# Masked attention over 256 keys: diagonal blocks side by side, the full block a product of its own

## The reference

```
L0_attn  scores = q k^T * scale + linear position bias; causal mask; softmax; times v   (16 channels a head)
L2_xattn q, k, v with low-rank additions; causal mask (T = S = 256); softmax; times v   (16 channels a head)
L3_attn  scores = (q_r k_r^T + q_i k_i^T) / sqrt(16); causal mask; softmax; times (v_r, v_i)   (32 a head)
```

## Time and profile before

| what | value |
|---|---|
| median of 3 runs | 3406.8 us (3401.21 to 3409.35) |
| the profiled execution | 3406.46 us |
| its span | 3404.6 us |
| TensorE busy | 2733.6 us, 80% |
| VectorE busy | 1700.3 us, 50% |
| ScalarE busy | 1108.8 us, 33% |
| mean granted TensorE clock | 0.864 |
| L0_attn, L2_xattn, L3_attn: first mask product | 740, 2268, 3044 us |

### The profile page before, as it was taken

One profiled execution on the slowest core, in us unless ns is written; L12 is line 12 of the kernel. 1 busy time (PEld: TensorE's weight loads), 2 busy tenths in 40 slices (PEclk: granted clock), 3 DMA queues, 4 the chain that ended last, 5 costly groups with the idle time before them and its releaser, 6 DMA issues. The chain is left out here.

```text
span 3404.6 us, 39821 instructions
## 1 busy us (share of the span) xinstructions
PE 2733.6 (80%) x15316; PEld 1488.6 (44%) x15320; DVE 1700.3 (50%) x2604; ACT 1108.8 (33%) x1564; POOL 191.8 (6%) x362
## 2 busy tenths in 40 slices
PE   3799599878999967998799759687684668978777
PEld 2233233335555544435343335434222555746446
DVE  5677477522111135774677287423697424322423
ACT  2466356512111112664366226211321113302220
POOL 2000100000000000000000045000000000000000
PEclk8799699987999978999899856798677788979888
DMA  4633443221221125431633000100100241020200
GB/s 156 145 54 50 113 105 57 32 76 38 74 74 70 41 87 131 80 58 21 162 59 58 24 10 1 47 24 1 51 0 0 99 158 52 1 77 1 81 1 7
DMA packets 89492, 202.14 MB, mean 59 GB/s; under 512 B 10770, under 2 KB 66322, under 8 KB 78354
## 3 DMA queue, kind: packets, MB, share of 16 engines
q1 hardware_dynamic: 85566, 184.09, 21.9%
q10 hardware_dynamic: 3750, 15.65, 1.2%
HBM read 171.56 MB, written 28.15 MB: 59 GB/s over the span
## 5 line engine op out<-in xcount | busy, mean ns | idle before, releaser
L589 DVE TENSOR_REDUCE sta_parts<-sta_psS 128x1 f32<-128x1024 f32 x544 | 644.1, 1191 | 250.3 <-PE sta_psS L519 241.8
L648 ACT ACTIVATE sta_probs<-sta_psS 128x1024 f32<-128x1024 f32 x544 | 543.0, 998 | 424.2 <-PE sta_psS L519 421.3
L519 PE MATMUL sta_psS<-L_xattna_kst,L_xattn_qS 99*128 99x512 bf16 x1088 | 339.2, 398 | 67.3 <-DMA L_xattna_kst<-ones_rows 61.3
L531 PE MATMUL sta_psO<-sta_probs,L_xattn_V 128*32 128x256 f32 x4224 | 368.3, 393 | 13.2 <-ACT sta_num L631 10.7
L519 PE MATMUL sta_psS<-L_xattn_qS,L_xattna_kst 99*128 99x256 bf16 x2112 | 325.4, 276 | 23.0 <-DVE L_xattn_qS L599 13.1
L519 PEld LDWEIGHTS sta_psS<-L_xattn_qS,L_xattna_kst 99*128 99x128 bf16 x2112 | 189.4, 98 | 200.2 <-DVE sta_parts L589 82.2
L519 PEld LDWEIGHTS sta_psS<-L_xattna_kst,L_xattn_qS 99*128 99x128 bf16 x1088 | 65.0, 99 | 286.0 <-issue 190.7
L531 PEld LDWEIGHTS sta_psO<-sta_probs,L_xattn_V 128*32 128x32 f32 x4224 | 95.9, 108 | 133.3 <-issue 89.6
L1298 DVE TENSOR_TENSOR l0f_hT<-exp_psG,l0f_gel 128x512 f32<-128x512 f32 x72 | 49.8, 692 | 204.5 <-PE exp_psG L1267 204.5
L199 ACT ACT_TABLE_LOAD x14 | 18.0, 1283 | 368.5 <-PEq L59 368.5
L1283 ACT ACTIVATE l0f_gel<-exp_psA 128x512 f32<-128x512 f32 x72 | 43.0, 597 | 275.5 <-PE exp_psA L1264 275.5
(11 more groups left out here) (578 smaller groups left out, 4312.7 us busy)
## 6 DMA issues: line engine op xcount, KB each, us to landing
L_xattna_kst<-L_xattn_keys SPq DMA_DIRECT2D x192, 136.0 KB
L_xattn_keys<-prt_parts SPq DMA_DIRECT2D x64, 384.0 KB, 2.6
L_xattna_kst<-L_xattn_keys SPq DMA_DIRECT2D x192, 128.0 KB
L_xattn_cx<-in_ctx SPq DMA_DIRECT2D x20, 1024.0 KB, 17.6
grp_W<-in_W SPq DMA_DIRECT2D x15, 1024.0 KB, 7.1
l0f_W<-in_W SPq DMA_DIRECT2D x12, 1024.0 KB, 7.1
grp_W<-in_M SPq DMA_DIRECT2D x10, 1024.0 KB, 7.5
l2f_W<-in_M SPq DMA_DIRECT2D x8, 1024.0 KB, 6.2
```

What stands on the lines that cost most here:

```text
L519: last = nc.tensor.matmul(psS[:, at % SLOTS, col:col + rhs.shape[1]], lhsT, rhs, start=True, stop=True)
L531: last = nc.tensor.matmul(psO[32 * group:32 * group + 32, 0, :], v, probs[:, u % NP, col:col + T], start=first, stop=final)
L589: nc.vector.tensor_reduce(into(parts[:, u // n % 2]), view(src), AX.X, ALU.max).then_inc(max_taken, 1)
L648: nc.scalar.activation(probs[:, g % NP, 0:cols], psS[:, place["score", g] % SLOTS, 0:cols], ACT.Exp, scale=scale).then_inc(probs_ready, 1)
```

## The change

The banks are laid out anew: columns 0 to 127 and 128 to 255 hold the two diagonal blocks, under a mask of two triangles (256 columns instead of 384), and columns 256 to 383 hold the full block (query tile 1, key tile 0), which gets no mask and a product of its own, issued behind the diagonal one of i = 1. For M the split is of the 256 keys of query tile 1, for S of the 256 queries of key tile 0. In L3_attn the lift product is split in the same way. The exponential and the maxima read the same 384 columns. The product with the values reads its first probabilities in two pieces of 128 columns. The table of constants is 128 columns narrower.

```diff
 def m_product(u, j, t):
     b, c, _ = where(u)
-    keys = (t + 1) * P if mask else T
-    return nc.tensor.matmul(psM[:, u % 2, j, t * SPLIT:t * SPLIT + keys], q[rows(u, j), c, b * T + t * P:b * T + (t + 1) * P],
-                            k[rows(u, j), c, b * T:b * T + keys], start=not mask, stop=t == TB - 1 or not mask)
+    queries = q[rows(u, j), c, b * T + t * P:b * T + (t + 1) * P]
+    if not mask:
+        return nc.tensor.matmul(psM[:, u % 2, j, t * T:(t + 1) * T], queries, k[rows(u, j), c, b * T:(b + 1) * T], start=True, stop=True)
+    one = nc.tensor.matmul(psM[:, u % 2, j, t * P:(t + 1) * P], queries, k[rows(u, j), c, b * T + t * P:b * T + (t + 1) * P],
+                           start=False, stop=t == 1)
+    if t:
+        one = nc.tensor.matmul(psM[:, u % 2, j, T:T + P], queries, k[rows(u, j), c, b * T:b * T + P], start=True, stop=True)
+    return one

 def s_product(u, j, kt):
     b, c, _ = where(u)
-    r, at, closed = rows(u, j), kt * P if mask else 0, kt == TB - 1 or not mask
-    dst = psS[:, j, kt * T:(kt + 1) * T - at]
-    one = nc.tensor.matmul(dst, k[r, c, b * T + kt * P:b * T + (kt + 1) * P], q[r, c, b * T + at:(b + 1) * T],
-                           start=not mask, stop=spare and closed)
+    r = rows(u, j)
+    keys = k[r, c, b * T + kt * P:b * T + (kt + 1) * P]
+    if not mask:
+        return nc.tensor.matmul(psS[:, j, kt * T:(kt + 1) * T], keys, q[r, c, b * T:(b + 1) * T], start=True, stop=True)
+    one = nc.tensor.matmul(psS[:, j, kt * P:(kt + 1) * P], keys, q[r, c, b * T + kt * P:b * T + (kt + 1) * P], start=False, stop=spare and kt == 1)
     if not spare:
-        one = nc.tensor.matmul(dst, K["lift"][r, :], lifted[r, u // 2 % 2, at:T], start=False, stop=closed)
+        one = nc.tensor.matmul(psS[:, j, kt * P:(kt + 1) * P], K["lift"][r, :], lifted[r, u // 2 % 2, kt * P:(kt + 1) * P], start=False, stop=kt == 1)
+    if kt:
+        one = nc.tensor.matmul(psS[:, j, T:T + P], k[r, c, b * T:b * T + P], q[r, c, b * T + P:(b + 1) * T], start=True, stop=spare)
+        if not spare:
+            one = nc.tensor.matmul(psS[:, j, T:T + P], K["lift"][r, :], lifted[r, u // 2 % 2, P:T], start=False, stop=True)
     return one
...
-nc.tensor.matmul(psM[:, m % 2, j, 0:W], K["ident16"], K["steps16_q"], start=True, stop=False)
+nc.tensor.matmul(psM[:, m % 2, j, 0:T], K["ident16"], K["steps16_q"], start=True, stop=False)
...
-nc.tensor.matmul(psS[:, j, 0:W], K["ident16"], K["steps16_k"], start=True, stop=False)
+nc.tensor.matmul(psS[:, j, 0:T], K["ident16"], K["steps16_k"], start=True, stop=False)
...
-last = nc.tensor.matmul(psO[row:row + HP, at:T], v[:, b * TB + kt, h * HP:(h + 1) * HP],
-                        probs[:, u % NP, j, kt * T:kt * T + T - at], start=kt == 0, stop=kt == TB - 1)
+weights = probs[:, u % NP, j, kt * T:(kt + 1) * T]
+if mask:
+    weights = probs[:, u % NP, j, P:T] if kt else probs[:, u % NP, j, :].rearrange("p (a n) -> p a n", a=2)[:, :, 0:P]
+last = nc.tensor.matmul(psO[row:row + HP, at:T], v[:, b * TB + kt, h * HP:(h + 1) * HP], weights,
+                        start=kt == 0, stop=kt == TB - 1)
...
-steps16 = p.sb("steps16", [P, 2, 3 * P], BF16)
+steps16 = p.sb("steps16", [P, 2, 2 * P], BF16)
```

More of the change, by code:

```diff
@@ L2318, in constants @@
         "mask_q": chunks(mask_q),
-        "steps": np.stack([np.concatenate([tri, 0 * tri, tri], axis=1) for tri in (mask_q[:P, :P], mask_q[:P, :P].T)], axis=1),
+        "steps": np.stack([np.concatenate([tri, tri], axis=1) for tri in (mask_q[:P, :P], mask_q[:P, :P].T)], axis=1),
     }
```

## The result

The changed kernel takes 3426.99 us (median of 6 runs, 3424.4 to 3440.68) beside 3408.33 for the kernel before: a ratio of 1.0058, interval 1.0037 to 1.0080. It is 18.7 us slower where 4 were forecast, and outside the range. The runs of the kernel before spread from 3401 to 3417, so single differences of a few us say little; the stages of a profile say more.

What follows compares the result with a forecast made beforehand. The three masked attention stages were taken as bound by TensorE, with short waits. Terms -0.5 (L0_attn), -0.5 (L2_xattn) and +4.95 (L3_attn) gave +3.95 us on 3406.46: 3410.4 us, range 3402 to 3417.

Steps and rivals of the forecast that it cites:

- The queue rule: TensorE's row strips: each takes two products (four passes), and in-order issue stops when a third comes; M1 waits 0.64 us.
- M1 would not have waited: L3_attn: what the skill's reorder window of 64 and pulled-ahead loads would imply, against the trace's 0.64 us wait.
- L3_attn, +4.95 us: L3_attn: pairs lose 0.55 us, seven at full clock 3.85 and the first at half clock 1.1, so 4.95 us slower.
- L0_attn and L2_xattn, -0.5 each: These two stages: a pair costs 0.23 and gains 0.298 us, 0.065 us x 8 pairs, 0.5 us gained in each.
- Values, 0: Values product reading its first weights in two pieces of 128 columns: 0 taken, 2 us either way kept for the range.
- Rival 1: All three stages: issue looks past a full strip, so the masks' whole 7.7 us gain stays: 3398.8 us; chance 9%.
- rival 3: Masked stages: mask gains go into waits and what is added stands alone, 11.6 us slower: 3418 us; chance 5%.
- The three units that have only M products at the start of each stage: Start of each masked stage: these units gain 0.107 and lose 0.107 us, so neither is taken.
- Rival 2: L3_attn's start: the lower clock lasts 13.7 us longer, costing 3.3 us plus 0.4 for added products: 3414.1 us; chance 14%.
- L2_xattn none in its steady part: L2_xattn: the profile rows show no lower clock in its steady part, against 6.8 us in L0_attn and 13.7 in L3_attn.
- the first 13.7 us of L3_attn: L3_attn: this stretch runs at clock 0.5, which rises after TensorE has been busy for 13.50 us of it.

Runs made afterwards that it cites:

- round robin: Changed kernel with full blocks in a third round over all strips and lift products behind the scores of both heads: 3405.78 us, ratio 0.9997.
- third round: Changed kernel with full blocks in a round of their own, but each lift product right behind its score: 3412.52 us, ratio 1.0006.
- lifts behind: Kernel before with only L3_attn's lift products moved behind the scores of both heads: 3406.48 us, ratio 0.9994.
- wide masks: Changed kernel with masks widened to 384 columns again (third block zeros), the full block's product adding to them: 3425.55 us, ratio 1.0044.
- whole ones: Changed kernel with the three M-only units opening each stage as in the kernel before (384-column masks, unsplit products): 3417.44 us, ratio 1.0020.

## Why the prediction was wrong, point by point

- *The queue rule* (two products a strip, a third stops the issue) was right. It was put on four new orders of products (the changed one, round robin, third round, lifts behind), on the changed one also with wide masks: pairs of 4.98, 7.98, 8.30, 5.27, 6.87, 4.74, 7.07 and 7.13 us came where the step, or the expectation drawn from it, gave 4.95, 7.9, 8.3, 5.24, 6.82, 4.71, 7.08 and 7.13. That the issue stops is shown; that the limit is counted in products and not in passes, no run tells apart, since each product has two passes. One thing beside it is read wrongly in the prediction: a start of matmuls in program order, which it names just before "M1 would not have waited", would have made M1 wait for S0's lift. The trace has no such order: in the unit of the earlier trace rows M1's first product starts at 3078.05, 0.5 us before S0's first lift (3078.57), which stands ahead of it.
- *L3_attn, +4.95 us*: 4.9 us up to the 15th exponential, with the clock taken out of the comparison. So close a hit has some luck in it: the pairs lost 0.64 us and not 0.55. *L0_attn and L2_xattn, -0.5 each*: the pairs gained 0.03 instead of 0.065 us, so -0.25. *Values, 0*: right.
- *Rival 1* (the issue looks ahead) and *rival 3* (masks' gain hidden): both refuted, by the loads of M1 (in L2_xattn the second comes 0.34 us after the unit's first load, where rival 1 needed 0.25 or less) and by the wide masks.
- *What failed* is that the sum was made with the clock as it stood in the trace of before. The step that names it is "The three units that have only M products at the start of each stage gain 0.107 and lose 0.107. Neither is taken." In time that is right. But in L2_xattn these units are where the clock is decided: with them it fell to 0.50 for 17.1 us, which cost 7.0 us. This had no term in the sum. Rival 2 says only that other stages "can also catch another clock", both ways, and gives it no size.
- *Rival 2* had the mechanism, but in L3_attn alone, at +3.7 us and 14%. Measured there: 9.1 us up to the 15th exponential (74.2 beside 65.1) less the 4.9 of the queue, so 4.2 us of clock; another 1.1 us come behind it, up to 10.2 for the stage. It was kept out of L2_xattn because the rows showed none there: "L2_xattn none in its steady part" was read as safety, while it was a stage with the same three lead units and the same 1.2 us of waiting at its start as the two that fell. The prediction also has "the first 13.7 us of L3_attn" at 0.5; the row starts at 3048.50, and the stage at 3044. Two lead units and the wait behind them had passed at 1.00 before the clock fell, so what precedes the fall was there to be looked at.
- *The range* was too narrow upwards for that reason: three stages have the same start, and each can lose some us to the clock (2 in L0_attn, 7 in L2_xattn, 5 in L3_attn here). These make up most of the 18.7 - 4 = some 15 us that were not forecast. That one cause moves all three is not shown.
- *Open*: how the low stretch in L3_attn comes to last 23.9 us and not 13.7. The changed lead units are not its cause (it lasts as long with whole ones, 108.5 us for the stage). Round robin, with the same columns, has 13.7 again and wide masks 17.1, which fits TensorE's strips standing idle in the changed order's units; an experiment that varies only this at low clock was not made. Open too is why L0_attn had 17.1 us at 0.50 in one profile of the changed kernel and 6.8 in the other.

## What to carry to other kernels

Before splitting products that run on row strips, write down the order strip by strip: here more than two products in a row on one strip held up the others, and the split issued in rounds over all strips cost at most 0.05 us a pair (4.74 us beside 4.71 and 6.87 beside 6.82, the pairs expected with no cost for the split). A change that thins out TensorE's work at the start of a stage, or beside a wait, should be priced with the start of the stage at half clock as well, also where the trace shows full clock. And a stage made faster at its start can lose it at its tail: compare stages up to their ends.

## What the runs showed that was not expected

The clock went by more than whether TensorE was busy. In the kernel before, the first 2.7 us of L2_xattn and what follows:

```profile
2267.60:2270.30 2.70, 2.62 (x20) 1.27 (x20) 1.02 (x2) 1.26 (x1) 0.52 (x1) 1.00 0.61 166
2270.30:2284.00 13.70, 11.46 (x126) 6.92 (x126) 6.91 (x15) 3.56 (x5) 0.00 (x0) 1.00 0.27 109
```

Busy for 2.62 of 2.70 us there, and the clock stays at 1.00 through the wait of 1.2 us that follows; the changed kernel was busy for 2.46 of 2.50, and it fell to 0.50. By the busy column the two are alike, and what differs is what the array was given in the two lead units of this stretch: four masks of 384 columns and eight whole products, or four of 256 columns and twelve split ones. Narrow masks are not needed for the fall: with wide masks and split products it came as well (0.50 for 13.7 us), and there the columns are those of the kernel before. So splitting the products is enough; whether narrow masks over whole products would be, no run tells. The other surprise is how exactly it repeats: in two profiles of each kernel the stretches at the start of L2_xattn and L3_attn lasted the same to 0.1 us, though the executions reached these stages up to 16 us apart.
